# A cross-attention's maximum pass moved into its key and value projection

## The chip, the cores and the metric

The kernel runs on one core of a Trainium2 chip. The metric is device microseconds (us) of one execution. TensorE (PE) multiplies matrices, VectorE (DVE), ScalarE (ACT) and GpSimd (POOL) work elementwise, SyncE (SP) issues most DMAs. Each engine takes its instructions in order, and engines wait for each other by semaphores.

## The reference, cut to what matters

Three layers on a stream x of 256 tokens by 512: cross-attention to a context of 4096 tokens, grouped self-attention, and a gated feed-forward layer. The change touches the first, and nothing of what the others compute:

```python
q = _qdq(x) @ _qdq(wq).T + bq                 # 256 x 512, int8 fake-quantized
kv = cond @ wkv.T + bkv                        # cond: 4096 x 512; wkv: 1024 x 512
k, v = jnp.split(kv, 2, axis=-1)               # 16 heads of 32
attn = jax.nn.softmax(jnp.einsum('bnhd,bmhd->bhnm', q, k) * scale, axis=-1)
o = jnp.einsum('bhnm,bmhd->bnhd', attn, v).reshape(B, N, C)
out = _qdq(o) @ _qdq(wp).T + bp
```

The result must keep nearly full fp32 precision. So each fp32 operand is split into a high part (fp32r, which TensorE multiplies in one pass) and a low part, and a product is three passes: high by high, high by low, low by high (`three_pass`).

## The kernel before, in words

**Stage A, keys and values.** The context comes in eight chunks of 512 tokens (`context_chunk`). ScalarE rounds a chunk to its high part (`high`), VectorE subtracts for the low part (`low`). TensorE projects four groups g of 128 key channels (four heads each; 12 matmuls of 512 columns each, PSUM banks 0 and 1), then four tiles mt of 128 tokens of values (12 matmuls each, banks 2 and 3). ScalarE writes the high part of the keys (L639), VectorE the low part (`k_low`, L878); both go to a scratch in DRAM, `kh_dram` and `kl_dram`. The values stay in SBUF as `v_all`, head by head (L653). During chunk 1 the queries are prepared: x is normalized and quantized, wq and wp are quantized in halves on VectorE (`quantize_weight_half`), transposed on TensorE, and the queries projected, split (`split_queries`) and stored.

**Stage B, sixteen heads.** For head h the high keys, low keys and high keys again are loaded from the scratch as three times 32 rows into one of two `k_stack` buffers, so that one matmul of 96 rows does the three passes at once (`load_k`); two rows of ones below them take the negated row maximum. The queries are loaded to `q_max` and `q_stack` in the same way.
- The maximum pass (`maximum_pass`, L1214): 16 matmuls a head, of 96 rows by 512 columns, queries on the output's partitions, into banks 4 and 5; VectorE reduces each (`chunk_maxima`, L918). It runs one head ahead, in pairs of tiles between the other matmuls. For head 0 it is spread over stage A.
- `negate_maximum`, `maximum_rows` (TensorE turns it into two rows, bank 7) and `maximum_row` (VectorE writes them to `q_stack`, L953).
- `scores` (L1307): eight chunks c of 512 keys, each four matmuls of 98 rows by 256 columns, keys on the output's partitions, into banks 0 and 1 or 2 and 3. ScalarE takes the exponential of a whole chunk, 128x1024, to a ring of four (`p_ring`, L681).
- `values` (L1319): four matmuls side by side in four column groups of 32, bank 6, from `v_head`, a copy of the head's values that a DMA makes of `v_all`.
- The softmax's denominators: GpSimd adds chunks 1, 2, 4, 5 and 6 to chunk 0 (`sum_chunks`, L563); TensorE multiplies chunks 3 and 7 and that sum by ones (`denominators`, L1331).
- ScalarE copies bank 6 out (L670), TensorE merges the four column groups (`merge`, L1293 and L1295), VectorE divides (`normalize_output`).

The order of the matmuls in a head is written out by hand in `head`: for i of 0 to 3, two maximum tiles, scores(2i), scores(2i+1), two maximum tiles, at i = 1 the merge of the head before, at i = 3 the maximum rows of the next one, then the values of the two chunks before.

An fp32 matmul stands in the trace as two records; an fp32r one as one.

Of the kernel before, what the change touches and what calls it, by code (L numbers as in the profile page):

```python
# [35 lines left out]
P = 128  # L36
# [10 lines left out]
SUM_CHUNKS = (0, 1, 2, 4, 5, 6)  # L47
NSUMS = len(SUM_CHUNKS) - 1
SUMS_BEFORE = (-2, -1, 0, None, 1, 1, 2, None)
# [23 lines left out]

FF_UNITS = 4
NSTREAM = FF0 + 3 * FF_UNITS

# [32 lines left out]
def perceiver(nc, x_in, stream, wq_in, wp_in, bias_cols, bias_rows, out):  # L109
    with ExitStack() as ctx:  # L110
# [17 lines left out]
        x_hat = sb("x_hat", [P, NT, D], F32)  # L128
# [17 lines left out]
        m_part = sb("m_part", [P, CHUNKS, NT], F32)  # L146
        neg_m = sb("neg_m", [P, NT], F32)
        neg_hl = sb("neg_hl", [P, NT, 2], F32)
# [5 lines left out]
        s_inv = sb("s_inv", [P, 2, NT], F32)  # L154


        with ExitStack() as ab:
            v_all = sb("v_all", [P, H, MT, DH], F32, ab)
            with ExitStack() as prep:
                w_raw = sb("w_raw", [P, 2, D], F32, prep)  # L160
                w_q = [sb(f"w_q{i}", [P, KT, D], BF16, prep) for i in range(2)]
                wq_t = sb("wq_t", [P, KT, D], BF16, prep)
                ones = sb("ones", [P, P], F32, prep)
                diag = sb("diag", [P, KT, P], F32, prep)
                sx_row = sb("sx_row", [P, N], F32, prep)
                in_q = sb("in_q", [P, NT, D], BF16, prep)
                in_t = sb("in_t", [P, KT, N], BF16, prep)
                w_amax = sb("w_amax", [P, KT], F32, prep)
                w_inv = sb("w_inv", [P, KT], F32, prep)
                wq_s = sb("wq_s", [P, KT], F32, prep)  # L170
                wp_s = sb("wp_s", [P, KT], F32, prep)

            k_stack = [sb("k_stack0", [P, M], F32R, ab)]
            q_max = [sb("q_max0", [P, N], F32R, ab)]
            q_stack = [sb("q_stack0", [P, N], F32R, ab)]
            q_max.append(sb("q_max1", [P, N], F32R, ab))
            q_stack.append(sb("q_stack1", [P, N], F32R, ab))
            v_head = [sb("v_head0", [P, MT, DH], F32, ab)]
            with ExitStack() as a:
# [5 lines left out]
                kl_buf = sb("kl_buf", [P, KT, D], F32R, a)  # L185
            with ExitStack() as b:
# [38 lines left out]
        def bank(i):  # L225
            return ps[:, i, :]


        wkv_raw = v_all[:].rearrange("p h m d -> p (h m d)")[:, 0:2 * KT * D].rearrange(
            "p (w k n) -> p w k n", w=2, k=KT)  # L230
        bp_row = swp_row
        q_f = diag[:, 0:NT, :].rearrange("p t n -> p (t n)")

# [1386 lines left out]
```

## Time and profile before

| | us |
|---|---|
| median of three runs | 686.84 (686.0 to 687.2) |
| the profiled execution: its time | 683.01 |
| its span, first to last instruction | 681.2 |
| busy in the span: TensorE | 619.2 |
| VectorE | 411.6 |
| ScalarE | 291.5 |
| GpSimd | 240.9 |

Mean granted TensorE clock: 0.962 of full speed. A group in the profile is all instructions of one line, engine, operation and form; its mean is of one instruction with its latency, so pipelined matmuls add up to more than their busy time. "idle" ahead of an instruction names the work that ended the wait. The lines L326 to L328 are the three passes of `three_pass`.

### The profile page before, as it was taken

The numbers are of one execution on the slowest core, as the hardware profiler recorded it, in microseconds if no ns is written. First come the engines' busy times: TensorE is split into PE (matmuls) and PEld (weight loads), VectorE is DVE, ScalarE is ACT, GpSimd is POOL, SyncE is SP. The second block draws the span as 40 slices with busy tenths as digits, with TensorE's granted clock in tenths as the row PEclk, the third lists the DMA queues.
The fourth block names the chain that finished last, engine by engine and source line by source line (L and its number), as shares of the span: only waits on it lengthen the run. The fifth ranks groups of instructions, "written<-read, shape, count | busy, mean of one in ns | idle before, by whom it ended". The sixth has DMA issues, their size and how long they took to land.

```text
span 681.2 us, 12389 instructions
## 1 busy us (share of the span) xinstructions
PE 619.2 (91%) x4324; PEld 479.7 (70%) x4324; DVE 411.6 (60%) x721; ACT 291.5 (43%) x392; POOL 240.9 (35%) x125
## 2 busy tenths in 40 slices
PE   5999999999999999999999999985796879779998
PEld 3877788888866666666666666653686768669997
DVE  3796432223347777777777777732478786765552
ACT  3444233323315455555444555452154446444441
POOL 1000200000026666777777777773002433230000
PEclk9999999999999999999999999976697999879999
DMA  8663644365294555555555555301031123125520
GB/s 301 242 228 131 221 147 147 123 209 170 99 278 117 138 135 146 151 142 137 145 145 145 143 141 136 85 8 55 1 125 62 63 98 150 62 74 201 184 99 31
DMA packets 29757, 92.17 MB, mean 135 GB/s; under 512 B 5472, under 2 KB 9568, under 8 KB 23008
## 3 DMA queue, kind: packets, MB, share of 16 engines
q1 hardware_dynamic: 28480, 89.67, 43.1%
q10 hardware_dynamic: 1248, 2.10, 0.8%
q8 instruction: 19, 0.31, 0.2%
q14 instruction: 10, 0.08, 0.0%
HBM read 65.02 MB, written 18.35 MB: 122 GB/s over the span
## 4 chain that ended last, share of the span: by engine, by line
PE 74%; DVE 12%; issue 6%; ACT 5%; POOL 1%; DMA 1%; SPq 0%; ACTq 0%; POOLq 0%; DVEq 0%
PE ps L326 13%; PE ps L327 13%; PE ps L328 13%; PE ps L1214 10%; PE ps L1319 9%; PE ps L1307 8%; PE ps L1331 3%; ACT p_ring L681 3%; DVE s_max L1046 1%; DVE s_bias L1048 1%; POOL p_sum L563 1%; DVE probs L1043 1%; PE ps L1293 1%; DVE probs L1054 1%; PE ps L1295 1%
## 5 line engine op out<-in xcount | busy, mean ns | idle before, releaser
L918 DVE TENSOR_REDUCE m_part<-ps 128x1 f32<-128x512 f32 (+1 forms) x256 | 165.4, 686 | 92.2 <-PE ps L1214 86.6
L681 ACT ACTIVATE p_ring<-ps 128x1024 f32<-128x1024 f32 x128 | 124.6, 1024 | 100.7 <-PE ps L1307 100.7
L563 POOL TENSOR_TENSOR p_sum<-p_sum,p_ring 128x1024 f32<-128x1024 f32 x64 | 152.6, 2384 | 13.4 <-ACT p_ring L681 9.2
L1214 PE MATMUL ps<-k_stack,q_max 96*128 96x512 f32 (+1 forms) x256 | 98.4, 439 | 3.4 <-DVE m_part L918 1.3
L1307 PEld LDWEIGHTS ps<-q_stack,k_stack 98*128 98x128 f32 x512 | 71.2, 191 | 18.6 <-ACT p_ring L681 11.3
L1307 PE MATMUL ps<-q_stack,k_stack 98*128 98x256 f32 x512 | 76.9, 288 | 7.8 <-ACT p_ring L681 7.8
L1319 PE MATMUL ps<-p_ring,v_head 128*32 128x256 f32 x1024 | 75.7, 391 | 0.1
L1214 PEld LDWEIGHTS ps<-k_stack,q_max 96*128 96x128 f32 x256 | 42.6, 188 | 42.7 <-issue 22.7
L326 PE MATMUL ps<-xt_h,h_ring 128*128 128x256 f32 x208 | 60.9, 293 | 2.2 <-DVE xt_l L1017 2.1
L563 POOL TENSOR_TENSOR p_sum<-p_ring 128x1024 f32<-128x1024 f32 x16 | 38.0, 2373 | 70.2 <-ACT p_ring L681 70.2
L878 DVE SCALAR_TENSOR_TENSOR kl_buf<-ps,biases,kh_buf 128x512 fp32r<-128x512 f32 x32 | 23.9, 749 | 61.3 <-ACT kh_buf L639 60.9
L327 PE MATMUL ps<-xt_l,h_ring 128*128 128x256 f32 x208 | 60.6, 291 | 0.0
L328 PE MATMUL ps<-xt_h,l_ring 128*128 128x256 f32 x208 | 60.4, 291 | 0.0
L326 PE MATMUL ps<-h_ring,wkv_h 128*128 128x512 f32 x128 | 52.0, 406 | 8.7 <-DVE l_ring L838 8.1
L309 DVE TENSOR_TENSOR l_ring<-f_ring,h_ring 128x2048 fp32r<-128x2048 f32 x22 | 51.7, 2354 | 12.6 <-ACT h_ring L305 12.5
L327 PE MATMUL ps<-l_ring,wkv_h 128*128 128x512 f32 x128 | 50.8, 397 | 0.0
L328 PE MATMUL ps<-h_ring,wkv_l 128*128 128x512 f32 x128 | 50.8, 397 | 0.0
L326 PE MATMUL ps<-wkv_h,h_ring 128*128 128x512 f32 x128 | 50.1, 391 | 0.0
L328 PE MATMUL ps<-wkv_h,l_ring 128*128 128x512 f32 x128 | 49.9, 390 | 0.0
L327 PE MATMUL ps<-wkv_l,h_ring 128*128 128x512 f32 x128 | 49.9, 390 | 0.0
L589 POOL TENSOR_TENSOR l_ring<-f_ring,h_ring 128x2048 fp32r<-128x2048 f32 x7 | 32.0, 4572 | 44.5 <-ACT h_ring L741 31.7
L653 ACT COPY v_all<-ps 128x512 f32 (+1 forms) x32 | 18.8, 587 | 67.0 <-PE ps L328 67.0
(174 smaller groups left out, 1034.7 us busy)
## 6 DMA issues: line engine op xcount, KB each, us to landing
f_ring<-stream SPq DMA_DIRECT2D x29, 1024.0 KB, 4.9
k_stack<-kh_scratch SPq DMA_DIRECT2D x60, 256.0 KB, 4.6
kh_scratch<-kh_buf SPq DMA_DIRECT2D x32, 256.0 KB, 5.6
kl_scratch<-kl_buf SPq DMA_DIRECT2D x32, 256.0 KB, 6.2
v_head<-v_all SPq DMA_DIRECT2D x16, 512.0 KB, 3.0
k_stack<-kl_scratch SPq DMA_DIRECT2D x30, 256.0 KB, 4.2
v_all<-stream SPq DMA_DIRECT2D x4, 256.0 KB, 4.9
f_ring<-stream SPq DMA_DIRECT2D x4, 256.0 KB, 5.6
```

What stands on the lines that cost most here:

```text
L309: nc.vector.tensor_tensor(l_ring[which][:], f_ring[which][:], h_ring[which][:].bitcast(F32), ALU.subtract).then_inc(l_ready, 1)
L326: nc.tensor.matmul(out_ap, lh, rh, start=start, stop=False)
L327: nc.tensor.matmul(out_ap, lh, rl, start=False, stop=False)
L328: return nc.tensor.matmul(out_ap, ll, rh, start=False, stop=stop)
L563: nc.gpsimd.tensor_tensor(p_sum[:, p, :], p_ring[:, 0, :] if n == 0 else p_sum[:, p, :], p_ring[:, c % 4, :], ALU.add).then_inc(sums_done, 1)
L589: nc.gpsimd.tensor_tensor(l_ring[w][:], f_ring[w][:], h_ring[w][:].bitcast(F32), ALU.subtract).then_inc(l_ready, 1)
L681: nc.scalar.activation(p_ring[:, c % 4, :], ps[:, 2 * (c % 2):2 * (c % 2) + 2, :].rearrange("p b n -> p (b n)"), ACT.Exp, scale=XSCALE).th ...
L878: nc.vector.scalar_tensor_tensor(out=kl_buf[:, g, :], in0=bank(g % 2), scalar=biases[:, KT + g:KT + g + 1], in1=kh_buf[:, g, :].bitcast(F3 ...
L918: nc.vector.reduce_max(m_part[:, mc0 + j // NT, j % NT:j % NT + 1], bank(4 + j % 2), AX.X).then_inc(max_read, 1)
L1214: nc.tensor.matmul(bank(to), q_max[p][0:SPLIT_ROWS, at128(j % NT)], k_stack[p][0:SPLIT_ROWS, k_at], start=True, stop=True).then_inc(max_do ...
L1307: last = nc.tensor.matmul(ps[:, 2 * (c % 2) + k // 2, (k % 2) * N:(k % 2 + 1) * N], k_stack[p][0:SPLIT_ROWS + MAX_ROWS, at128(4 * c + k)], ...
L1319: last = nc.tensor.matmul(bank(6)[k * DH:(k + 1) * DH, 0:N], v_head[p][:, 4 * c + k, :], p_ring[:, c % 4, k * N:(k + 1) * N], start=c == 0 ...
```

## The change

- The maximum pass leaves stage B. In stage A there are now 64 sets: for chunk c, group g of four heads and query tile t, twelve matmuls of 32 rows by 512 columns, three passes over four heads; head i takes partitions 32i to 32i+31 of the keys and queries as they lie in SBUF, and bank 4 + i. One maximum on VectorE reads the four banks. A set waits for the maximum of the set before.
- Stage A is a list of half steps (6 matmuls): values of chunks 0 and 1, then keys of chunks 0, 1 and 2, and from there values and keys in turn. `SETS_AFTER` says after which of the 112 half steps a set stands: the first sixteen after steps 5 to 16 and 18 to 21, the rest from 23 on nearly evenly, most of them two steps apart.
- The low parts of the context from chunk 2 on, and that of the keys' weights, move from VectorE to GpSimd.
- wq is quantized before the key steps, wp between maxima in steps 24 to 38, and wp is transposed after step 45.
- In stage B, VectorE adds chunks 0 to 6 (six adds, `add_chunk`), and TensorE makes denominators of chunk 7 and the sum only. `v_all` is laid out token tile first and read by `values` directly; `v_head` and its loads are gone, and so are `q_max` and its loads. Output accumulates in bank 6 or 4 in turn. The maximum rows of head h+1 are made at i = 2, and VectorE copies them to `q_stack` behind its sixth add.
- Loops over chunks and heads on TensorE are unrolled.

```diff
-SUM_CHUNKS = (0, 1, 2, 4, 5, 6)
-NSUMS = len(SUM_CHUNKS) - 1
-SUMS_BEFORE = (-2, -1, 0, None, 1, 1, 2, None)
+NSUMS = 6
+SUMS_BEFORE = (-2, -1, 0, None, 1, 1, 2, 3)
...
+SETS = KT * NT
+FIRST_SETS = (5, 6, 7, 8, 9, 10, 11, 12, 13, 14, 15, 16, 18, 19, 20, 21)
+STEPS = 2 * KT * (2 * NCTX - 2)
+WP_STEP = 45
...
+def step_before_set(m):
+
+    if m < len(FIRST_SETS):
+        return FIRST_SETS[m]
+    c, g = m // SETS, m % SETS // NT
+    even = 23 + (m - 16) * (STEPS - 24) // (SETS * NCTX - 17)
+    return max(even, first_step_of_keys(c) + 2 * g + 3)
...
+            def context_low(s, w):
+                pool.wait_ge(h_ready, s + 1)
+                pool.wait_ge(l_ready, s)
+                nc.gpsimd.tensor_tensor(l_ring[w][:], f_ring[w][:], h_ring[w][:].bitcast(F32),
+                                        ALU.subtract).then_inc(l_ready, 1)
...
+            def set_maxima(m):
+                c, g, t = m // SETS, m % SETS // NT, m % NT
+                dve.wait_ge(max_done, m + 1)
+                nc.vector.reduce_max(m_part[:, c, t, g * HPG:(g + 1) * HPG], ps[:, 4:8, :], AX.X).then_inc(max_read, 1)
...
+            for step in range(STEPS):
+                kind, c, g, half = step_of(step)
+                if kind == "k" and half == 1:
                     k_low(c, g)
...
+                if step == 3:
+                    split_queries()
+                for m in SETS_AFTER[step]:
+                    set_maxima(m)
...
+            def add_chunk(h, p, c):
+
+                dve.wait_ge(exp_done, 8 * h + c + 1)
+                if c == 1:
+                    wait(dve, sums_used, h - 1)
+                else:
+                    dve.wait_ge(sums_done, NSUMS * h + c - 1)
+                nc.vector.tensor_tensor(p_sum[:, p, :], p_ring[:, 0, :] if c == 1 else p_sum[:, p, :],
+                                        p_ring[:, c % 4, :], ALU.add).then_inc(sums_done, 1)
+
+            def head(h, p):
+
+                first, last = (isinstance(h, int) and h == n for n in (0, H - 1))
+                for c in range(1, 4):
+                    add_chunk(h, p, c)
                 if not first:
                     normalize_output(h - 1)
...
+                add_chunk(h, p, 4)
                 if not first:
                     output_maximum(h - 1)
...
+                for c in range(5, 7):
+                    add_chunk(h, p, c)
+                if not last:
                     maximum_row(h + 1, 1 - p)
...
+            def maximum_set(m):
+
+                c, g, t = m // SETS, m % SETS // NT, m % NT
+                pe.wait_ge(kl_evac, 4 * c + g + 1)
+                if m == 0:
+                    pe.wait_ge(ql_ready, KT)
+                wait(pe, max_read, m)
+                for n, (q, k) in enumerate(((q_nat_h, kh_buf), (q_nat_h, kl_buf), (q_nat_l, kh_buf))):
+                    for i in range(HPG):
+                        rows = slice(i * DH, (i + 1) * DH)
+                        last = nc.tensor.matmul(bank(4 + i), q[rows, g, at128(t)], k[rows, g, :],
+                                                start=n == 0, stop=n == 2)
+                last.then_inc(max_done, 1)
...
+            def head(h, p):
 
                 for i in range(4):
...
+                    scores(h, p, 2 * i)
+                    scores(h, p, 2 * i + 1)
+                    if i == 1 and h > 0:
                         merge(h - 1)
-                    if i == 3 and next_loads is not None:
+                    if i == 2 and h < H - 1:
                         maximum_rows(h + 1)
                     if i > 0:
-                        values(h, p, loads, 2 * i - 2)
-                        values(h, p, loads, 2 * i - 1)
-                    elif not first:
-                        values(h - 1, 1 - p, None, CHUNKS - 2)
-                        values(h - 1, 1 - p, None, CHUNKS - 1)
+                        values(h, p, 2 * i - 2)
+                        values(h, p, 2 * i - 1)
+                    elif h > 0:
+                        values(h - 1, 1 - p, CHUNKS - 2)
+                        values(h - 1, 1 - p, CHUNKS - 1)
```

## Rows read from the trace of the kernel before

**Rows 1.** The page: busy us of TensorE, share of the span, instructions.

```profile
PE 619.2 (91%) x4324; PEld 479.7 (70%) x4324; DVE 411.6 (60%) x721; ACT 291.5 (43%) x392; POOL 240.9 (35%) x125
```

**Rows 2.** Windows of stage A and B: length, then busy us of each engine.

```profile
core 0: us, PE busy (x) PEld busy (x) DVE busy (x) ACT busy (x) POOL busy (x), PEclk, DMA share, GB/s
64.00:203.99 139.99, 137.97 (x603) 112.19 (x602) 50.23 (x67) 40.16 (x54) 7.04 (x2) 1.00 0.55 173
222.35:434.96 212.61, 205.56 (x1926) 138.44 (x1925) 156.29 (x326) 107.45 (x119) 154.63 (x65) 1.00 0.54 141
```

**Rows 3.** TensorE's timeline in stage A; 48 matmuls lie between the starts.

```profile
22.73 0.39 PE L326 MATMUL ps<-wkv_h,h_ring 128*128 128x512 f32 x1
...
33.61 0.39 PE L326 MATMUL ps<-h_ring,wkv_h 128*128 128x512 f32 x1
```

**Rows 4.** ScalarE's timeline over one head (start, us, what, idle before).

```profile
304.38 2.88 ACT L681 ACTIVATE p_ring<-ps 128x1024 f32<-128x1024 f32 x3
309.72 1.94 ACT L681 ACTIVATE p_ring<-ps 128x1024 f32<-128x1024 f32 x2 [2.45 <-PE ps L1307]
...
320.75 1.03 ACT L681 ACTIVATE p_ring<-ps 128x1024 f32<-128x1024 f32 x1
```

**Rows 5.** VectorE's timeline: query split (first, last), a maximum row, the last normalization.

```profile
63.19 0.48 DVE L865 SCALAR_TENSOR_TENSOR diag<-ps,wq_s,sx_row 128x256 f32<-128x256 f32 x1 [1.73 <-PE ps L1206]
...
68.39 0.48 DVE L871 SCALAR_TENSOR_TENSOR o_all<-diag,biases,x_hat 128x256 fp32r<-128x256 f32 x1
...
315.51 0.43 DVE L953 CAST q_stack<-ps 2x256 fp32r<-2x256 f32 x1
...
468.98 0.17 DVE L958 RECIPROCAL r_den<-ps 128x2 f32<-128x2 f32 x1 [10.90 <-PE ps L1295]
```

**Rows 6.** TensorE's timeline inside one head.

```profile
308.39 0.73 PE L1214 MATMUL ps<-k_stack,q_max 96*128 96x512 f32 x2
308.96 1.12 PE L1307 MATMUL ps<-q_stack,k_stack 98*128 98x256 f32 x8
309.92 0.85 PE L1214 MATMUL ps<-k_stack,q_max 96*128 96x512 f32 x2
310.70 1.07 PE L1319 MATMUL ps<-p_ring,v_head 128*32 128x256 f32 x16
...
318.26 1.07 PE L1319 MATMUL ps<-p_ring,v_head 128*32 128x256 f32 x16
...
320.13 0.74 PE L1214 MATMUL ps<-k_stack,q_max 96*128 96x512 f32 x2
```

**Rows 7.** Groups by form: count, busy us, mean ns of one, idle before.

```profile
L918 DVE TENSOR_REDUCE m_part<-ps 128x1 f32<-128x512 f32 x244 | 157.1, 686 | 66.9 <-PE ps L1214 61.3
L589 POOL TENSOR_TENSOR l_ring<-f_ring,h_ring 128x2048 fp32r<-128x2048 f32 x7 | 32.0, 4572 | 44.5 <-ACT h_ring L741 31.7 <-ACT h_ring L305 12.7
L346 DVE TENSOR_REDUCE w_amax<-w_raw 128x2 f32<-128x1024 f32 x2 | 2.4, 1213 | 0.0
L887 DVE TENSOR_TENSOR wkv_l<-v_all,wkv_h 128x2048 fp32r<-128x2048 f32 x1 | 2.3, 2291 | 1.0 <-ACT wkv_h L643 1.0
L910 DVE TENSOR_TENSOR x_cur<-x_cur,swp_row 128x512 f32<-128x512 f32 x2 | 1.4, 692 | 0.1
```

**Rows 8.** Windows, columns as in rows 2; PEclk is the granted clock.

```profile
452.00:458.00 6.00, 6.00 (x39) 4.09 (x43) 4.46 (x5) 2.51 (x3) 4.22 (x3) 0.50 0.01 3
508.00:512.00 4.00, 1.98 (x16) 1.61 (x16) 3.45 (x11) 2.19 (x8) 0.00 (x0) 1.00 0.00 2
```

**Rows 9.** TensorE's timeline in the last head, with idle time before.

```profile
448.84 0.64 PE L1331 MATMUL ps<-p_sum,ones_col 128*32 128x256 f32 x8 [0.94 <-POOL p_sum L563]
...
451.11 0.80 PE L1307 MATMUL ps<-q_stack,k_stack 98*128 98x256 f32 x4 [0.97 <-ACT p_ring L681]
...
455.20 2.08 PE L1307 MATMUL ps<-q_stack,k_stack 98*128 98x256 f32 x8
```

**Rows 10.** Groups of weight loads by form, columns as in rows 7.

```profile
L1214 PEld LDWEIGHTS ps<-k_stack,q_max 96*128 96x128 f32 x256 | 42.6, 188 | 42.7 <-issue 22.7 <-DVE m_part L918 18.9 <-DMA k_stack<-kh_scratch 0.4
L1319 PEld LDWEIGHTS ps<-p_ring,v_head 128*32 128x32 f32 x1024 | 31.5, 110 | 20.1 <-issue 8.0 <-ACT p_ring L681 1.1
```

More of the change, by code:

```diff
@@ new lines, in next_chunk_high @@
+            def next_chunk_high(c):
+                act.wait_ge(k_done, 4 * min(c, 2))
+                act.wait_ge(v_done, 4 * c)
+                high(act, c + 3, slot(c + 3), uses(c + 3))
+            high(act, CTX0 + 1, 1, 1)
+            for mt in range(4):
+                evacuate_values(0, mt)
+            act.wait_ge(wk_loaded, 16)
+            nc.scalar.copy(wkv_h[0][:], wk_raw).then_inc(h_ready, 1)
+            evacuate_values(1, 0)
+            evacuate_values(1, 1)
+            evacuate_tokens(0, in_t)
@@ L908, in _ @@
-            dve.wait_ge(rows_loaded, 32)
-            for t in range(NT):
-                order.step(nc.vector.tensor_tensor(x_cur[:, t, :], x_cur[:, t, :], bp_row[:], ALU.add))
-            weight_and_token_rows()
-            split_queries()
-            def chunk_maxima(h, first, last, mc0=0):
-                for j in range(first, last):
-                    dve.wait_ge(max_done, 16 * h + 2 * mc0 + j + 1)
-                    nc.vector.reduce_max(m_part[:, mc0 + j // NT, j % NT:j % NT + 1], bank(4 + j % 2),
-                                         AX.X).then_inc(max_read, 1)
@@ L1209, in project_queries @@
                         last.then_inc(q_done, 1)
-            def maximum_tile(j, to, k_at, p, before):
-                wait(pe, max_read, before - 1)
-                nc.tensor.matmul(bank(to), q_max[p][0:SPLIT_ROWS, at128(j % NT)], k_stack[p][0:SPLIT_ROWS, k_at],
-                                 start=True, stop=True).then_inc(max_done, 1)
-            def maximum_pass(h, p, loads, first, last):
-                for j in range(first, last):
-                    if j == 0:
-                        pe.wait_ge(qm_loaded[p], 48 * loads)
-                    if j % 8 == 0:
-                        pe.wait_ge(ks_loaded[p][j // 8], 48 * (loads - 1 + p))
-                    maximum_tile(j, 4 + j % 2, slice(j // NT * D, (j // NT + 1) * D), p, 16 * h + j)
@@ new lines, in _ @@
+            transpose_wq()
+            split_chunk(CTX0 + 1)
+            for step in range(STEPS):
+                kind, c, g, half = step_of(step)
+                if kind == "k":
+                    if c >= 2 and g == 0 and half == 0:
+                        split_chunk(c + CTX0)
+                    project_keys(c, g, half)
+                else:
+                    project_values(c, g, half)
+                if step == 1:
+                    project_queries()
+                for m in SETS_AFTER[step]:
+                    maximum_set(m)
+                if step == WP_STEP:
+                    prepare_wp(sum(len(sets) for sets in SETS_AFTER[:step + 1]))
+                if step == STEPS - 4:
+                    maximum_rows(0)
@@ L1375, in _ @@
+            pe.wait_ge(ones_set, 3)
+            pe.wait_ge(max_read, SETS * NCTX)
+            for h in range(H):
+                head(h, h % 2)
             for c in (CHUNKS - 2, CHUNKS - 1):
-                values(H - 1, 1, None, c)
-            pe.wait_ge(o_done, NT * (H - 1))
+                values(H - 1, 1, c)
             merge(H - 1)
```

586 lines of the change are left out of this document (248 added, 338 removed).

## The prediction

> **What bounds the kernel now.** I read the page first, then the windows by stage, then TensorE's timeline at the start and the three engines' timelines inside one head, then the groups by form, for what one instruction costs, and last the granted clock where TensorE idles. TensorE is busy 619.2 of 681.2 us [rows 1], but the stages differ. Stage A (keys and values, up to the first scores at 203.99) is projection back to back: TensorE busy 137.97 of 139.99 us [rows 2]; 48 matmuls of 512 columns take 10.88 us, 0.227 us each [rows 3]. Stage B (sixteen heads) is also TensorE's, 205.56 of 212.61 us, with VectorE at 156.29, ScalarE at 107.45 and GpSimd at 154.63 [rows 2]. A head repeats every 16.37 us (exponentials at 304.38 and 320.75, [rows 4]). The last normalization of stage B is at 468.98 [rows 5], so B lasts 265.0 us. What follows, 212 us, is unchanged. So the question is what A gains in length and what B loses.
>
> In a head, two chunks of scores cost 0.96 us, two maximum tiles before them 0.57, two before values 0.78, and two chunks of values with two sets of denominators 1.87 [rows 6]. The 16 tiles are thus some 5.5 to 6 us, the rest some 10.4.
>
> **Stage B after.** Gone are the maximum tiles, one of three denominator sets (0.4 us), the loads of q_max and v_head (hidden today) and GpSimd's adds. TensorE keeps about 10 us per head, ScalarE eight exponentials at 0.97 and a copy, 8.3. VectorE gets six adds of 128x1024. Between 692 ns for 512 and 2291 for 2048 elements [rows 7] an add is 1.22 us; each waits for the one before, so 1.24. With the normalization (0.75), the output maximum (0.25) and the maximum row (0.43, [rows 5]) that is 8.9 us: less than TensorE's, but it is a chain. Two SBUF operands are taken at the same rate in both of these rows, so I see no reason for an add outside 1.14 (next to no wait) to 1.36. The new wait is that scores(h+1, 0) needs maximum_row(h+1), which now stands behind add 6 of head h on VectorE. By hand, from the start of scores(h, 0) as 0:
> - exponential 0 starts at 0.75 (308.96 to 309.72, [rows 4, 6]), exponential 1 ends at 2.67;
> - TensorE does both scores, the old head's last values and denominators by 2.9, scores 2 follow, and exponential 2 runs from 3.65 to 4.61, behind the copy;
> - VectorE: add 2 at 4.67, add 3 to 7.1, normalization to 7.9, add 4 to 9.1, maximum, add 5 to 10.6, add 6 to 11.8 (exponential 6 ended at 9.8), maximum row to 12.25.
>
> The next scores start at 12.3. Fifteen such periods and 14.2 us for the last head up to its normalization are 198.7 us: B loses 66. Behind the wait stand the old head's last values, so TensorE idles some 2.2 us in each head (10.05 to 12.3). Bounds: 10.7 if the row came free (TensorE and ScalarE taking turns), 13.0 if an add costs 1.36. DMA is hidden: today's 55% of 16.37 us is 9 us, under 12.3 even with nothing removed.
>
> **Stage A after.** The 96 matmuls of the two value chunks end at 33.61 as today's first chunk does [rows 3]; I add 1.1 for the low part of chunk 1, 2.0 for transposes and 1.2 until wq is rounded: the key steps start at 37.9 (36 to 40). A half step is 6 x 0.227 = 1.36 us.
> - Steps 0 to 5 and the query projection: 9.9, to 47.8. Queries are split after the second low part of the keys, from 46.2, for 5.7 us (63.19 to 68.88, [rows 5]), so the first set waits until 52.0.
> - A set is 12 matmuls of 32 rows, in three rounds over four row groups, into banks 4 to 7, and one maximum of 4 x 512 elements. By 686 ns for 512 and 1213 for 1024 [rows 7] that takes 2.27 us. The banks are single: matmuls of set m+1 wait for the maximum of set m, and behind that wait, in TensorE's queue, stands the next half step of the projection, and so the evacuations and the key stores that follow it. Four matmuls into four column groups do run side by side today: 16 records in 1.07 us [rows 6]. If row groups do too, a round costs 0.227, the set occupies TensorE 0.68 plus 0.17 for changing shape (0.78 against 0.57, [rows 6]), 0.85; from release to last result it is 1.04.
> - So sets follow each other no faster than 1.04 + 0.06 + 2.27 + 0.07 = 3.44 (0.06 and 0.07 are my estimate of what passes between two engines). With one half step between them TensorE has only 2.21 us of work: 1.2 is idle. Sets 0 to 16: 14 such gaps and 2 of two steps (3.6) are 55.4, to 107.4.
> - Sets 16 to 63 (the schedule's own list): 40 gaps of two steps at 3.6, six tight at 3.44, one of three at 4.95, the last set 1.05: 170.6, to 278.0.
> - Preparing wp with its two copies in line 4, wp's rounding between maxima 2, last maximum 2.3: scores start near 286, not 204. A grows by 82.
>
> The low parts that move to GpSimd (4.57 us each, [rows 7]) and to ScalarE's copy have a chunk of over 40 us to hide in; without that cover each would be 4.6. The values' copy keeps its size and only its order of writing changes: nothing. SP's queue loses 48 small loads of q_max, the sixteen of v_head and their waits; k_stack for head h+2 has a head and a half to land, 16 us and more, so its queue is no bound. Writing the query parts to q_nat_h and q_nat_l instead of two older buffers is the same work: nothing.
>
> Two tiles before column groups cost 0.2 us more than two before full-array scores [rows 6]. The Trainium skill, TensorE Tiling, Tiling Modes, says why: TensorE drains when the tiling mode changes. The sets make 128 such changes; by that rule and this row they would be 26 us against my 11, and the sum 744.
>
> **The clock.** The granted clock was 1.00 through stage B, but in the last head it stood at 0.50 (1.2 of 2.4 GHz) from 452 to 458 [rows 8], after idle gaps of 0.94 and 0.97 us a little apart [rows 9]; it held from 508 to 512, where TensorE was busy 1.98 us of 4 [rows 8]. The new 2.2 us idle of every head lie between these two. At half clock eight scores take 2.08 instead of 1.12 [rows 6, 9]. A fall right behind the gap of 3.5 to 6.8 us doubles up to 2.9 us of TensorE work before exponential 2, and with it the chain: 1.75 to 3.2, so 2.4. I take 11 of 16 heads: 26 us (bounds 0 and 51).
>
> **Sum, against the profiled execution's 683.01 us:** +82 - 66 + 26 = +42, 725; the runs' median is 3.8 higher, so 729.
>
> **Rivals.**
> 1. *Loads in single file.* A 32-column load takes 110 ns, one of 128 columns 188, though it has 96 rows and not 128 [rows 10]: 0.81 ns per column, 0.104 us for 128, and nothing for rows. If loads of different row groups queue, 12 x 0.107 (with a little for the start) = 1.28: TensorE 1.45 per set, 1.75 to the result, tight gaps 4.15, double 4.25. Sets 0 to 16 take 66.5, sets 16 to 63 202.2, scores start at 329, A grows by 125: 683 + 125 - 66 = 742, or 746 as a median; 772 with clock falls. For it: each set brings 12 full-width loads for 0.68 us of streaming. Against: nothing here shows loads queueing at that rate.
> 2. *Clock holds*, as in 508 to 512: 683 + 82 - 66 + 4 = 703. For it: a head is still 10 us of work in 12.3.
> 3. *No overlap at all* between row groups: 12 x 0.227 = 2.73 per set, 64 x 1.9 = 121 more: 824 and up. The column groups speak against it.
> 4. *Faster: the heads get short.* If the maximum row is not late, because adds keep up with the exponentials, a head is 10.7 and the idle gap goes, the clock with it: 16 x 1.6 = 26 below rival 2, 677. It decides from a head under 11.2 us (16 us / 16) with sets at 0.85. For it: VectorE has only 8.9 us of work. Against: add 3 to the maximum row is an unbroken row of steps.
>
> TensorE: Matmul & The Clock Gate, Part 3, in the Trainium skill, reports 3.07 times for four row tiles of 512 columns. By that a round would be 4 x 0.227 / 3.07 = 0.30, and 64 sets 13 us more, an estimate; no run here shows it yet.
>
> **Chances.** Forecast 0.34 (own range 712 to 745); clock holds 0.17, of which 0.03 lands within 0.2%; loads in file 0.28; no overlap 0.04; faster 0.17. A difference of 0.2% is about what a measurement of this kernel can tell from none. Faster 0.17, same 0.03, slower 0.80. Range 680 to 775: it leaves out no overlap, the worst of rival 1 and the better half of rival 4.
>
> **What would show it.** Scores first start near 286 (330 under rival 1). Starts of four matmuls of a set 0.06 us apart, rounds 0.23 apart (0.43 under rival 1, 0.9 under rival 3). The maximum: near 2.27 us, and TensorE waiting for it some 1.2 us per set early on. Heads 12.3 apart at full clock, over 14 with falls; scores waiting for the maximum row (L953's successor) about 2 us per head; granted clock below 1.00 in stage B. The prediction is wrong if sets overlap with their own loads even less, if the idle gap does not lower the clock, or if adds run faster than 1.24.

## The result: 751 us instead of 687

| | us |
|---|---|
| before, median of 4 runs | 686.66 (686.0 to 687.2) |
| after, median of 4 runs | 750.88 (748.31 to 754.47) |
| ratio, 95% interval | 1.094 (1.088 to 1.100) |
| predicted | 729 (680 to 775), slower with 0.80 |

The profiled execution of after has a span of 746.5 us. The windows cut it at the first scores (before 203.99 [rows 2], now 313.21) and at the last normalization of stage B (before 468.98 [rows 5], now 535.16); those within stage A set apart the start, the first sets, and the stop from 165 to 177 in which TensorE prepares wp:

```profile
core 0: us, PE busy (x) PEld busy (x) DVE busy (x) ACT busy (x) POOL busy (x), PEclk, DMA share, GB/s
0.00:57.80 57.80, 40.05 (x174) 30.61 (x174) 36.13 (x55) 19.57 (x27) 12.96 (x24) 0.94 0.51 186
57.80:116.00 58.20, 45.80 (x312) 29.25 (x312) 44.07 (x27) 9.59 (x11) 9.15 (x2) 0.97 0.38 135
116.00:165.00 49.00, 44.71 (x284) 30.02 (x276) 41.27 (x38) 8.85 (x13) 4.60 (x1) 1.00 0.26 84
165.00:177.00 12.00, 8.97 (x44) 5.74 (x45) 2.38 (x2) 3.57 (x5) 0.00 (x0) 0.72 0.00 0
177.00:313.21 136.21, 127.24 (x797) 86.89 (x795) 93.74 (x62) 27.03 (x36) 21.97 (x5) 1.00 0.35 113
313.21:535.16 221.95, 190.03 (x1980) 130.22 (x1980) 136.38 (x176) 135.29 (x145) 0.00 (x0) 0.91 0.45 107
535.16:746.50 211.34, 175.69 (x1127) 156.77 (x1128) 135.56 (x210) 88.90 (x157) 38.68 (x21) 0.92 0.27 97
```

Stage A grew by 109 us, stage B shrank from 265 to 222, the rest kept its 211 to 212. TensorE, busy 619.2 us before [rows 1], is busy 632.5 now, and idle 52 us more. The longer busy time is not more work: with the same instructions and a granted clock of 0.99 instead of 0.91 in stage B, run 1 below is busy 619.6 us. The page says where the idle time is:

```profile
L885 DVE TENSOR_REDUCE m_part<-ps 128x4 f32<-128x2048 f32 x64 | 146.5, 2289 | 60.8 <-PE ps L1228 60.7
L973 DVE TENSOR_TENSOR p_sum<-p_sum,p_ring 128x1024 f32<-128x1024 f32 x80 | 98.0, 1225 | 32.6 <-ACT p_ring L677 28.2
L1315 PE MATMUL ps<-q_stack,k_stack 98*128 98x256 f32 x512 | 86.0, 316 | 33.6 <-DVE q_stack L899 30.5
```

TensorE waited 30.5 us before scores (L1315) for VectorE's copy of the maximum row (L899): the wait that the prediction put at 2.2 us a head. One head, first TensorE, then VectorE (start, us, what, idle before):

```profile
353.24 1.22 PE L1315 MATMUL ps<-q_stack,k_stack 98*128 98x256 f32 x8 [2.12 <-DVE q_stack L899]
...
366.07 1.99 PE L1315 MATMUL ps<-q_stack,k_stack 98*128 98x256 f32 x8 [2.12 <-DVE q_stack L899]
```

```profile
356.15 1.23 DVE L973 TENSOR_TENSOR p_sum<-p_ring 128x1024 f32<-128x1024 f32 x1 [2.97 <-ACT p_ring L677]
358.31 2.48 DVE L973 TENSOR_TENSOR p_sum<-p_sum,p_ring 128x1024 f32<-128x1024 f32 x2 [0.94 <-ACT p_ring L677]
360.83 0.17 DVE L955 RECIPROCAL r_den<-ps 128x2 f32<-128x2 f32 x1
...
361.50 1.22 DVE L973 TENSOR_TENSOR p_sum<-p_sum,p_ring 128x1024 f32<-128x1024 f32 x1
362.65 0.21 DVE L963 TENSOR_REDUCE a_part<-o_all  x1
363.07 2.48 DVE L973 TENSOR_TENSOR p_sum<-p_sum,p_ring 128x1024 f32<-128x1024 f32 x2 [0.21 <-DVE a_part L963]
365.59 0.43 DVE L899 CAST q_stack<-ps 2x256 fp32r<-2x256 f32 x1
```

The last line is what scores wait for, and everything above it from 358.31 on is a row of steps with no wait over 0.21 us. Scores start 12.83 us after those of the head before when the clock holds; before the change a head repeated every 16.37 [rows 4]. Both idle gaps are 2.12 us, but behind the second eight scores take 1.99 us and not 1.22: half clock (1.2 of 2.4 GHz), and the next copy comes 14.37 us later (379.96). Windows behind the first gap and behind the second show it in PEclk, the last but two of the figures:

```profile
353.00:357.00 4.00, 3.76 (x46) 2.71 (x47) 1.03 (x2) 2.52 (x3) 0.00 (x0) 1.00 0.47 98
366.00:370.00 4.00, 3.93 (x32) 2.73 (x36) 0.56 (x2) 1.94 (x2) 0.00 (x0) 0.57 0.45 94
```

Of the fourteen distances between the rows of heads 1 to 15, six are 12.5 to 12.8, seven 14.4 and one 15.8.

Then stage A. Two sets that are two half steps apart (a double gap), and two that are one apart (a tight gap):

```profile
233.72 0.50 PE L1228 MATMUL ps<-kh_buf,q_nat_h 32*128 32x512 f32 x4
234.06 0.40 PE L1228 MATMUL ps<-kl_buf,q_nat_h 32*128 32x512 f32 x4
234.30 0.40 PE L1228 MATMUL ps<-kh_buf,q_nat_l 32*128 32x512 f32 x4
234.62 0.50 PE L355 MATMUL ps<-wkv_h,h_ring 128*128 128x512 f32 x1
...
237.62 0.50 PE L1228 MATMUL ps<-kh_buf,q_nat_h 32*128 32x512 f32 x4
```

```profile
69.57 0.51 PE L1228 MATMUL ps<-kh_buf,q_nat_h 32*128 32x512 f32 x4 [0.90 <-DVE m_part L885]
...
73.02 0.51 PE L1228 MATMUL ps<-kh_buf,q_nat_h 32*128 32x512 f32 x4 [0.89 <-DVE m_part L885]
```

A line with x4 is one round over four heads, and the rounds start 0.34 and 0.24 us apart: four matmuls run in the time of one. The double gap is 3.90 (3.89 over many), the tight one 3.45 with 0.9 idle.

### The profile page after: what moved, and what is told of

Read it like the earlier page. It is cut to its first block, busy times and chain, and to the rows that moved or that the text cites. A ratio compares the mean times of both kernels' runs of the same rounds, so it can differ in the third digit from the quotient of the medians.

```text
span 746.5 us, 12075 instructions
## 1 busy us (share of the span) xinstructions
PE 632.5 (85%) x4707; PEld 469.5 (63%) x4708; DVE 489.5 (66%) x565; ACT 292.8 (39%) x392; POOL 87.4 (12%) x53
## 4 chain that ended last, share of the span: by engine, by line
PE 54%; DVE 28%; issue 10%; ACT 4%; DMA 2%; DVEq 1%; ACTq 0%; POOL 0%; SPq 0%
PE ps L355 12%; PE ps L356 11%; PE ps L357 11%; PE ps L1228 7%; DVE m_part L885 7%; PE ps L1315 6%; DVE p_sum L973 6%; PE ps L1327 4%; ACT p_ring L677 2%; PE ps L1339 2%; DMA x_cur<-x_in 2%; DVE probs L1055 1%; DVE s_max L1047 1%; DVE s_bias L1049 1%; DVE probs L1044 1%
## 5 line engine op out<-in xcount | busy, mean ns | idle before, releaser
L885 DVE TENSOR_REDUCE m_part<-ps 128x4 f32<-128x2048 f32 x64 | 146.5, 2289 | 60.8 <-PE ps L1228 60.7
L973 DVE TENSOR_TENSOR p_sum<-p_sum,p_ring 128x1024 f32<-128x1024 f32 x80 | 98.0, 1225 | 32.6 <-ACT p_ring L677 28.2
L1315 PE MATMUL ps<-q_stack,k_stack 98*128 98x256 f32 x512 | 86.0, 316 | 33.6 <-DVE q_stack L899 30.5
L1315 PEld LDWEIGHTS ps<-q_stack,k_stack 98*128 98x128 f32 x512 | 71.9, 208 | 61.8 <-DVE q_stack L899 37.7
L1327 PE MATMUL ps<-p_ring,v_all 128*32 128x256 f32 x1024 | 82.8, 423 | 0.0
L625 ACT ACTIVATE kh_buf<-ps,biases 128x512 fp32r<-128x512 f32 x32 | 22.0, 688 | 125.5 <-PE ps L357 125.5
L619 ACT COPY v_all<-ps 128x512 f32<-128x512 f32 x32 | 18.8, 586 | 97.8 <-PE ps L357 97.8
L1228 PE MATMUL ps<-kh_buf,q_nat_h 32*128 32x512 f32 x256 | 32.3, 491 | 26.2 <-DVE m_part L885 21.7
L973 DVE TENSOR_TENSOR p_sum<-p_ring 128x1024 f32<-128x1024 f32 x16 | 19.6, 1226 | 49.6 <-ACT p_ring L677 49.6
L334 ACT CAST h_ring<-f_ring 128x2048 fp32r<-128x2048 f32 x23 | 43.8, 1906 | 9.3 <-PE ps L357 7.2
L1327 PEld LDWEIGHTS ps<-p_ring,v_all 128*32 128x32 f32 x1024 | 33.1, 117 | 19.8 <-issue 4.8
```

Source lines behind the costliest of these rows:

```text
L334: nc.scalar.copy(h_ring[which][:], f_ring[which][:]).then_inc(h_ready, 1)
L625: nc.scalar.activation(kh_buf[:, g, :], bank(g % 2), ACT.Identity, bias=biases[:, KT + g:KT + g + 1]).then_inc(kh_evac, 1)
L885: nc.vector.reduce_max(m_part[:, c, t, g * HPG:(g + 1) * HPG], ps[:, 4:8, :], AX.X).then_inc(max_read, 1)
L973: nc.vector.tensor_tensor(p_sum[:, p, :], p_ring[:, 0, :] if c == 1 else p_sum[:, p, :], p_ring[:, c % 4, :], ALU.add).then_inc(sums_done, 1)
L1228: last = nc.tensor.matmul(bank(4 + i), q[rows, g, at128(t)], k[rows, g, :], start=n == 0, stop=n == 2)
L1315: last = nc.tensor.matmul(ps[:, 2 * (c % 2) + k // 2, (k % 2) * N:(k % 2 + 1) * N], k_stack[p][0:SPLIT_ROWS + MAX_ROWS, at128(4 * c + k)], ...
```

## The experiments

Runs 3 to 8 were executed once each. The changed kernel's own four times lie between 748.3 and 754.5, and in the four profiled executions whose stage A is that of the changed kernel (it, runs 1, 2 and 8) the first scores start between 313.21 and 316.10. So a difference of some 3 us in either, in a single run, shows nothing.

**1. The row earlier.** On VectorE one call moves:

```diff
                 if not first:
                     normalize_output(h - 1)
+                if not last:
+                    maximum_row(h + 1, 1 - p)
                 add_chunk(h, p, 4)
...
-                if not last:
-                    maximum_row(h + 1, 1 - p)
```

> One line moves: on VectorE the copy of the next head's maximum row stands right behind the normalization, before add 4, and no longer behind add 6. Nothing is left out. My theory (the scores of head h+1 wait for this row, and the idle gap of about 2 us that this makes lowers the clock): the row is there some 4 us before it is wanted, TensorE and ScalarE take turns, heads come 10.5 to 11 us apart instead of 12.6 and 14.4 in turn, the granted clock stays at 1.00 through the heads, stage B takes 15 x 10.7 + 14.2 = 175 us instead of 222, and the whole about 704. Rival 1 (the wait only moves: the last denominators of head h still need add 6, and TensorE idles there instead): heads about 12, stage B about 194, the whole about 723, clock still below 1.00. Rival 2 (the clock falls for another cause than the gap): heads 11 but with half-clock stretches, stage B about 195. Stage A unchanged in all: first scores at about 313.

Measured: 707.8 us (706.8 to 709.0), ratio to before 1.032 (1.027 to 1.037). The rows are 11.3 apart at first and 10.86 from the fourth on, and stage B, from 316.10 to 493.54, is 177.4 us. Its window:

```profile
316.10:493.54 177.44, 175.70 (x1980) 121.85 (x1980) 137.54 (x176) 135.05 (x145) 0.00 (x0) 0.99 0.57 133
```

(For the changed kernel the same window has 190.03 of 221.95 us and a clock of 0.91.) TensorE is idle for 1.7 of 177 us, and the granted clock is 0.99. So the order on VectorE alone costs 43 us; rival 1 (the wait only moves) and rival 2 (another cause of the clock) both fall.

**2. The gap filled.** Seven matmuls without use in the place of the wait:

```diff
+                    if i == 3 and h < H - 1:
+                        wait(pe, o_done, NT * h)
+                        for _ in range(7):
+                            nc.tensor.matmul(bank(7), h_ring[0][:, 0, 0:P], h_ring[0][:, 1, :], start=True,
+                                             stop=True)
```

> The wait for the maximum row stays, but TensorE gets seven matmuls of 512 columns (1.6 us, results unused, into a free bank) in each head behind values 5, where it now idles for 2.1 us. Nothing is left out, work is added. Theory (the gap lowers the clock, and that is what parts heads of 14.4 us from heads of 12.6): granted clock 1.00 in the heads, all heads 12.3 to 12.8 apart, stage B about 203 instead of 222, the whole about 732, although TensorE does 26 us of work more. Rival (the clock falls for another reason, or the clock is not what makes every second head long): heads stay at 12.6 and 14.4, or get longer by up to 1.6, the whole 751 to 775. Stage A unchanged.

(Their operands are a chunk for the second layer, waited for before the first head.) Measured: 735.9 us, 15 less than the changed kernel although TensorE gets 15 x 7 x 0.2325 = 24 us of work more.

```profile
402.54 1.91 PE L1364 MATMUL ps<-h_ring 128*128 128x512 f32 x7
404.73 1.22 PE L1315 MATMUL ps<-q_stack,k_stack 98*128 98x256 f32 x8 [0.28 <-DVE q_stack L899]
```

Scores still start when the row comes, the rows are 12.83 apart in nearly every head, and stage B has a granted clock of 0.99. The idle gap lowers the clock, and the clock is worth 15 us. What is left between this run and the one before (28 us; 15 heads by 12.83 - 10.86 are 29.6) is the wait itself.

**3. Another order in the set.** The two loops of `maximum_set` change places:

```diff
-                for n, (q, k) in enumerate(((q_nat_h, kh_buf), (q_nat_h, kl_buf), (q_nat_l, kh_buf))):
-                    for i in range(HPG):
+                for i in range(HPG):
+                    for n, (q, k) in enumerate(((q_nat_h, kh_buf), (q_nat_h, kl_buf), (q_nat_l, kh_buf))):
```

> The two loops of a set are swapped: the three passes of one head (one row group) follow each other, then the next head, so that neighbouring matmuls mostly share their row group; same number, shape and banks. Nothing is left out. Theory (matmuls of different row groups run side by side, those of one row group do not): the three passes of a head take 0.68 us, only the borders between heads overlap, a set occupies TensorE for 2.1 to 3.0 us instead of 1.16, double gaps grow from 3.89 to about 5.3, tight gaps from 3.46 to about 5.0, and the first scores start 60 to 110 us later, at 375 to 425. Rival (what overlaps is only the load with the matmul, and the four banks, not row groups): nothing changes, first scores at 313. Stage B unchanged in both.

Measured: 754.1 us, first scores at 318.13. My theory expected 375 to 425 and is wrong. (Of the 4.9 us against 313.21, 1.5 lie in the start, 1.5 in one gap of 5.89 instead of 4.35, which run 8 has too, and the rest in sets that are 0.02 to 0.05 longer.)

```profile
232.79 0.53 PE L1228 MATMUL ps<-kh_buf,q_nat_h 32*128 32x512 f32 x4
233.12 0.43 PE L1228 MATMUL ps<-kl_buf,q_nat_h 32*128 32x512 f32 x4
233.35 0.43 PE L1228 MATMUL ps<-kh_buf,q_nat_l 32*128 32x512 f32 x4
233.71 0.50 PE L355 MATMUL ps<-wkv_h,h_ring 128*128 128x512 f32 x1
```

The first matmuls of all four heads still start together, although two other matmuls of the first head stand ahead of that of the second in the program. A set takes 0.92 us from its start to the next projection (0.90 in the other order). Whether the row groups matter at all was now open.

**4. One row group.** All twelve matmuls read rows 0 to 31:

```diff
-                        rows = slice(i * DH, (i + 1) * DH)
+                        rows = slice(0, DH)
```

> All twelve matmuls of a set read rows 0 to 31 of the keys and queries, one row group, and still write four banks: three quarters of the maxima are left out (those of the first head of each group are taken four times). Number, shape, loads and banks are as in the changed kernel. Theory (the matmuls run side by side because they stand in four row groups; the order of issue did not matter): they now run one behind the other, a set takes 12 x 0.227 = 2.7 us and more, double gaps grow from 3.89 to 5.5 to 6, tight gaps from 3.46 to 5.2 to 5.6, first scores at 415 to 435, the whole about 855 to 870. Rival (what makes four run at once is that they are short of rows, or write four banks): double gaps stay at 3.89, first scores at 313, the whole 750. In between (a set of 1.3 to 2 us): loads overlap, streams do not.

Measured: 940.9 us, first scores at 506.84. From TensorE's timeline, and the window up to the copy of the first maximum row, 6 us before the scores:

```profile
303.55 1.19 PE L1228 MATMUL ps<-kh_buf,q_nat_h 32*128 32x512 f32 x4
304.59 1.07 PE L1228 MATMUL ps<-kl_buf,q_nat_h 32*128 32x512 f32 x4
305.50 1.08 PE L1228 MATMUL ps<-kh_buf,q_nat_l 32*128 32x512 f32 x4
306.51 0.80 PE L355 MATMUL ps<-wkv_h,h_ring 128*128 128x512 f32 x1
307.10 0.63 PE L356 MATMUL ps<-wkv_l,h_ring 128*128 128x512 f32 x1
```

```profile
0.00:500.83 500.83, 475.81 (x1587) 338.85 (x1587) 215.28 (x178) 68.08 (x89) 48.25 (x32) 0.79 0.22 76
```

The set takes 2.96 us instead of 0.90: with loads, shapes and four banks unchanged, what makes four matmuls run side by side is that they stand in four row groups. The mechanism and the size of the set (2.7 "and more") are as expected. The total is 70 us past my range, because behind many such sets the projection runs at half clock (0.43 us from matmul to matmul behind 307.10): the granted clock up to 500.83 is 0.79, with TensorE busy 476 of 501 us. Double gaps are 5.9 us where the clock holds, as expected (5.5 to 6), and 7.5 where it has fallen. I had not priced that.

**5. Full rows.** A set of four matmuls with the projection's own shape:

```diff
+                for i in range(HPG):
+                    last = nc.tensor.matmul(bank(4 + i), q_nat_h[:, g, at128(t)], (kh_buf, kl_buf)[i % 2][:, g, :],
+                                            start=True, stop=True)
```

> A set is four matmuls of 128 rows x 512 columns, of the same shape as the projection's, instead of twelve of 32 rows: the four banks then hold no head's scores, so the real maxima are left out. Streaming time 4 x 0.23 = 0.92 us against 3 x 0.23 = 0.69 in the set of the change, which occupies TensorE for 1.16. Theory (0.3 to 0.5 us of a set are the two changes between 128-row and 32-row matmuls): a set of full rows costs 0.92 and no changes, so double gaps get shorter than 3.89, 3.64 to 3.7, and the 40 of them about 9 us. Rival 1 (a set pays for something other than the shape, its start on new banks or its wait): double gaps get longer, 3.89 + 0.23 = 4.1. Tight gaps stay at 3.46 in both (the maximum's).

Measured: 745.3 us. Most double gaps are 3.71 to 3.73, tight ones 3.64. The lines at a set:

```profile
233.01 0.40 PE L1226 MATMUL ps<-kh_buf,q_nat_h 128*128 128x512 f32 x1
...
233.70 0.40 PE L1226 MATMUL ps<-kl_buf,q_nat_h 128*128 128x512 f32 x1
233.93 0.40 PE L355 MATMUL ps<-wkv_h,h_ring 128*128 128x512 f32 x1
```

Sixteen matmuls of one shape at 0.2325 are 3.72: no cost beyond the columns. The real set has three rounds, 0.70, but takes 3.89 - 12 x 0.2325 = 1.10. So 0.40 us of each set, 26 us of 64, go to the two changes of shape. That it is not the four row groups getting in each other's way is seen in run 4, whose twelve matmuls run one by one: the starts on either side of a change are 0.33 to 0.34 apart there too, and all others 0.23. I was wrong on the tight gaps: the maximum waits for a set that is 0.2 longer, and they grow with it.

**6. A shorter maximum.** VectorE reads a quarter of each bank (`ps[:, 4:8, 0:P]`).

> VectorE's maximum of a set reads 128 of the 512 columns of each bank: it leaves three quarters of the maxima out. It should take about 0.7 us instead of 2.29. Theory (the tight gaps of 3.46 are the maximum's, the double gaps of 3.89 are TensorE's: two half steps 2.72 and the set 1.16): tight gaps fall to 2.5 (1.36 + 1.16), double gaps stay at 3.89, about 20 tight gaps and the wait around the preparation of wp give 19 to 23 us, first scores at 290 to 294, the whole about 730. Rival 1 (the single banks or VectorE set the double gaps too): they fall as well, by up to 0.5 us each, first scores near 270. Rival 2 (the set itself costs TensorE less than it seems, since it only waits): tight gaps fall to 2.2 or less. Stage B unchanged.

Measured: 727.0 us, first scores at 288.75; the maximum takes 0.69.

```profile
232.94 0.69 DVE L885 TENSOR_REDUCE m_part<-ps 128x4 f32<-128x512 f32 x1 [1.34 <-PE ps L1228]
...
236.84 0.69 DVE L885 TENSOR_REDUCE m_part<-ps 128x4 f32<-128x512 f32 x1 [0.84 <-PE ps L1228]
```

Double gaps stay at 3.90, tight gaps are 2.97 and 2.03 in turn, 2.5 on average. Tight gaps are VectorE's, double ones TensorE's. Some 20 of them and the stop for wp gave 24 us.

**7. VectorE and GpSimd at the start.** Set 0 stood at 58.63 and not at 52.0. VectorE, then GpSimd, in the changed kernel:

```profile
25.87 4.68 DVE L385 TENSOR_SCALAR v_all<-v_all 128x512 f32<-128x512 f32 x1
30.59 3.70 DVE L387 TENSOR_SCALAR v_all<-v_all 128x512 bf16<-128x512 f32 x1
```

```profile
25.51 4.76 POOL L541 TENSOR_TENSOR wkv_l<-v_all,wkv_h 128x2048 fp32r<-128x2048 f32 x1 [5.95 <-ACT wkv_h L638]
30.40 3.61 POOL L544 MEMSET k_stack<- 32x4096 f32 x1
```

```diff
+            dve.wait_ge(h_ready, CTX0 + 2)
+            nc.vector.tensor_tensor(wkv_l[0][:], wk_raw, wkv_h[0][:].bitcast(F32), ALU.subtract).then_inc(l_ready, 1)
...
                 context_low(s, slot(s))
+                if s == CTX0 + 2:
+                    pool.wait_ge(ones_set, 1)
+                    pool.wait_ge(l_ready, CTX0 + 3)
+                    nc.gpsimd.memset(k_stack[0][SPLIT_ROWS:P, :].bitcast(F32), 1.0).then_inc(ones_set, 1)
```

> Two pieces of GpSimd work leave the stretch in which VectorE prepares the queries and weights: the low part of the key weights (4.76 us on GpSimd at 25.51) goes to VectorE, between the diagonals and the weights' scales (2.3 us there), and the filling of the ones rows of k_stack0 (3.61 us at 30.40) stands behind the first low part of a context chunk. Nothing is left out. Theory (VectorE's steps at 25.87 and 30.59 took 4.68 and 3.70 us instead of 0.43 because GpSimd ran beside them): both take about 0.43 again, transposes of the tokens are 5 to 6 us earlier, the idle gap of 5.5 us on TensorE before 34.35 and its half clock go, key steps start at 38 to 40 instead of 43.8, the queries are split and the first set starts at 52 to 54 instead of 58.6, first scores at 306 to 309, the whole about 745. Rival (the long steps wait for data, a transfer or something of their own): they stay near 4 us, and the 2.3 us more on VectorE make the first set later, 60 to 61, the whole 752 to 754.

Measured: 749.9 us. Both steps are short again:

```profile
26.13 0.43 DVE L385 TENSOR_SCALAR v_all<-v_all 128x512 f32<-128x512 f32 x1
26.59 0.43 DVE L387 TENSOR_SCALAR v_all<-v_all 128x512 bf16<-128x512 f32 x1
```

So the cause is shown: VectorE stood still while GpSimd's instruction ran, and each step ended 0.3 us after GpSimd's. The Trainium skill (SBUF — State Buffer, SBUF: two separate sides) has the rule: the two engines share a pair of ports that one of them holds for a whole instruction; VectorE wants it in a 2-port perf mode, or with two SBUF inputs against a GpSimd instruction that reads SBUF. The trace agrees that the wait lasts for the whole instruction (4.76 and 3.61 us); in which mode a step ran, no run here shows. Only 2.0 us come out at the first scores (311.22), not 4 to 7, and the total can't show so little. TensorE still waits, for wq (2.70) and as before for the split queries (4.45), behind one VectorE step too many. The 2.0 also understate the repair: in this execution GpSimd's first step on the tokens (L519) stood at 19.34 and not at 17.77, so everything behind the tokens began 1.6 us late.

**8. The adds back on GpSimd.** With them the copy of the maximum row goes right behind the normalization, and TensorE's merge waits for the normalization of the head before.

```diff
+            for h in range(H):
+                for c in range(1, 7):
+                    pool.wait_ge(exp_done, 8 * h + c + 1)
...
+                    nc.gpsimd.tensor_tensor(p_sum[:, h % 2, :], p_ring[:, 0, :] if c == 1 else p_sum[:, h % 2, :],
+                                            p_ring[:, c % 4, :], ALU.add).then_inc(sums_done, 1)
```

> The six adds of the chunks in a head go back to GpSimd, everything else of the change stays; the copy of the next head's maximum row then stands right behind the normalization on VectorE. Nothing is left out. What my account of the heads says: GpSimd's add takes 2.38 us, as before the change, six in a chain 14.3 us, with handoffs 14.6 to 16; the row is never late, the gap before the scores goes, and TensorE instead waits for the sums before the last denominators. Heads 14.6 to 16 us apart, stage B 235 to 255 instead of 222, the whole 760 to 785: moving the adds was worth some 15 to 35 us, less than what the order on VectorE gives (the run with the row earlier: 43). Rival (the length of a head comes from the other parts, the scores' exponentials and TensorE, and the adds have slack on GpSimd): heads 11 to 12, the whole about 710. Stage A unchanged.

Measured: 783.4 us; heads 15.3 apart on average, but mostly 12 and 17 to 19 in turn, and the granted clock from the first scores to the last normalization is 0.83. GpSimd, then TensorE's longest wait in a head:

```profile
380.79 12.41 POOL L570 TENSOR_TENSOR p_sum<-p_sum,p_ring 128x1024 f32<-128x1024 f32 x5 [0.30 <-ACT p_ring L688]
```

```profile
393.26 1.08 PE L1346 MATMUL ps<-p_sum,ones_col 128*32 128x256 f32 x8 [3.98 <-POOL p_sum L570]
```

Six adds in a row take GpSimd 14.8 us, so its chain alone makes heads long; how much of the rest is the clock was not taken apart. VectorE's adds, with their late row, are 32 us better than six adds on GpSimd, clock included, and with an early row 76. (Before, GpSimd had five.)

**9. Five repairs together.** Runs 1 and 7, queries split one key tile earlier (`if step == 1`), TensorE waiting for the prepared wp only at the next set (wp's transposes stand one half step later for it), and the wait for the last maximum moved from the first scores to the first values.

> Five small repairs of what the runs before showed, nothing left out: the maximum row stands right behind the normalization (707.8 us by itself); the low part of the key weights on VectorE and the ones rows filled later (first scores 2 us earlier by itself); the queries are split right behind the first low part of the keys and not the second (the first set waited 4.45 us for them); TensorE waits for the prepared wp only before the next set (an interval of 11.9 us between two maxima where 3.9 is usual); the wait for the last maximum stands before the first values and no longer before the first scores (2.45 us idle). My account (these waits add up, each is on TensorE's path): 707.8 - 2 - 4.4 - 5 - 3 = 693, first scores at 300 to 303, heads 10.86 apart. Rival (stage A is held by the maxima and not by TensorE, so an earlier start and a shorter stop are lost again in later tight gaps): first scores at 306 to 309, the whole 698 to 702. Against the kernel before, 686.7: slower by 1 to 2 per cent in both.

Measured: 689.6 us, ratio to before 1.007 (1.004 to 1.010). First scores at 298.52; the interval at wp is 7.06 instead of 11.91. All of the gain arrives, and some 3 us more. It lies in the start: the first maximum stands at 51.27, 10.9 us before that of run 1 (62.20), where 2 and 4.4 had been reckoned.

**10. Stage A in quarters.** The list of half steps becomes one of quarters (`.`), sets (`|`) and the rest (W, Q, P: wq, queries, wp; H: next chunk's high part; R: row of head 0). It was laid out with prices from the traces: 0.70 a quarter, 1.10 a set, 2.29 a maximum.

```diff
+PROGRAM = ("k00.... k01.... k02.W... k03.Q...H v13.... k10.|..|. v20..|.. v21.|...| k11...|. k12..|.. "
...
-                for kt in (2 * half, 2 * half + 1):
+                for kt in (quarter,):
```

> The repairs of the row, the low part and the last wait as in the combined run, and stage A in another order, nothing left out: the projection goes in quarters (three matmuls, 0.70 us) instead of halves of a tile, key and value tiles alternate in an order written out by hand, one value tile of chunk 1 stands behind the keys of chunk 0, and a set comes wherever VectorE is about to be free (every 3 or 4 quarters). Arithmetic, banks and buffers are those of the change. My account (tight gaps cost 0.94 us of idle TensorE each, 20 of them, because a half step of 1.36 us and a set do not fill 3.46; with quarters 3 x 0.70 + 1.16 = 3.25 nearly does): adding up quarters at 0.70, sets at 1.10 and maxima at 2.29 in this order gives the first scores at 287 and some 21 us of idle left, the whole 707.8 - (316.1 - 287) = 679, 1 per cent below the kernel before. Rival (stores, conversions of the next chunk or evacuations, which the halves had time for, now come late, or each change between tile shapes costs more than 1.10 allows): first scores at 295 to 305, the whole 687 to 697, no gain over the kernel before.

Measured: 676.3 us (675.8 to 680.0), ratio to before 0.987 (0.984 to 0.990): 1.3 per cent faster than the kernel before. First scores at 286.62. Windows of its three stages:

```profile
0.00:286.62 286.62, 263.65 (x1600) 180.70 (x1601) 213.86 (x184) 67.79 (x89) 43.85 (x31) 1.00 0.38 129
286.62:462.83 176.21, 174.56 (x1981) 120.86 (x1979) 136.87 (x173) 135.42 (x146) 0.00 (x0) 1.00 0.60 141
462.83:675.50 212.67, 175.31 (x1128) 156.61 (x1128) 137.58 (x210) 88.41 (x157) 38.71 (x21) 0.92 0.27 97
```

From set 30 on nearly every maximum starts 3.45 or 3.46 behind the last. There stage A is held by the chain of set and maximum over single banks; at 3.46 a set, 64 sets would be 221 us of it.

## Why the prediction was right, and where it was off

Slower was right, and by the mechanism named: A had to grow by more than B lost, because a set and its maximum follow each other over the same four banks. The 22 us that are missing are all in A. The number alone would not show it: 751 lies outside the forecast's own range (712 to 745) and nearer to rival 1's 746. What speaks for the forecast is its mechanism, row by row.

| term | predicted | measured |
|---|---|---|
| first maximum starts | 53.1 | 60.05 |
| sets 0 to 16 | 55.4 | 56.8 |
| sets 16 to 63, with wp | 169.6 + 6 | 193.9 |
| first scores | 286 | 313.21 |
| stage B with the clock | 198.7 + 26 | 222.0 |
| the rest | 212 | 211.3 |

- **The start (+7).** "The key steps start at 37.9 (36 to 40)"; they started at 43.8. The step that failed is that low parts on GpSimd have cover and cost nothing. They had it, but that of the key weights (4.76 us), and the filling of the ones rows behind it (3.61), stopped VectorE, which had none (run 7). I had asked what hides GpSimd's work, and not whom it slows. The half clock that the idle gap left on TensorE belongs to it.
- **Tight gaps.** 3.44 predicted, 3.45 measured; the maximum 2.27 and 2.29. Right, and run 6 shows that they are VectorE's.
- **Double gaps (+8).** 3.6 predicted, 3.89 measured, in 29 of the 47 distances from set 16 on. The rounds were right (0.227 predicted), the change of shape was not: 0.17 a set against 0.40 (run 5). The Trainium skill, TensorEngine Tiling (Array Packing), Tiling Modes, has the rule that a change of tiling mode drains TensorE. The trace agrees. The prediction's estimate with that rule, 26 us for 128 changes by its rows on column groups, is what 64 x 0.40 give; its sum took 11. Of these 26 only what falls into double gaps costs time.
- **Odd gaps and wp (+10).** Eleven distances are neither tight nor double, 57.0 us with the one at wp. At 3.6 each and one 4.95 they would be 41; the 6 us set aside for wp cover less than half of the rest. At wp the interval is 11.91, 8.0 over a double one: TensorE waited 2.49 for a maximum, did the transposes, waited for their copies and then ran four microseconds at half clock. The others lie where a set waits for the low part of its own keys or for wp's rounding, and I took apart only one. In the gap of 5.62 behind 135.92 the step that failed at the start fails again: GpSimd's low part runs from 136.01 for 4.60 us, and a VectorE step of 0.17 us for wp (L374, 139.37) takes 1.27 and ends with it.
- **Stage B (-3), by two errors that cancel.** A head at full clock is 12.83 and not 12.3: VectorE's chain is as long as worked out, to 0.1 us, but it starts 5.07 behind the scores (358.31 to 353.24) and not 4.67. The clock costs 15 us and not 26: it falls in about eight of the heads, and a fall costs 1.55, not 2.4 (run 2). Run 1 shows that both hang on one wait.
- **Rival 1** (loads in single file): refuted, rounds are 0.24 apart and not 0.43. (Its double gap should have been 2 x 1.36 + 1.45 = 4.17 and not 4.25, some 3 us less.) **Rival 3** (no overlap) is what run 4 made: 941 us. **Rival 2** (the clock holds) is run 2, and did not come by itself. **Rival 4** had the condition right (heads under 11.2), and one moved call brings 10.86; but it needed sets at 0.85 as well, so even then the kernel is 3 per cent slower than before.
- The rule that four row tiles give 3.07 times (the Trainium skill, TensorE: Matmul & The Clock Gate, Part 3) would make a round 0.30. The trace disagrees for rounds that follow each other within a set (0.24) and lies near it for a whole set: 2.96 / 0.90 = 3.3.

## What to carry to other kernels

Work that is moved to an idle engine must be priced twice: its own time, and what it does to the engine beside it. Where a product and its reduction pass through one set of banks, their sum is a period, and the work between two of them should be cut into pieces that fill it; here quarters instead of halves, with keys and values in turn, turned 0.7 per cent slower into 1.3 per cent faster, the new order taken as a whole. And a result that another engine waits for goes ahead of the work that only a later step needs: one line, 43 us.

## What was not expected of the hardware

- The order in which matmuls of different row groups are issued made no difference (0.92 and 0.90 us a set): in the trace the fourth head's first matmul starts with the first head's, ahead of six that stand before it in the program. So "each engine takes its instructions in order", as said at the beginning, does not hold for TensorE's starts across row groups.
- The granted clock fell to its lower level (1.2 GHz) behind sets of twelve matmuls in one row group, with TensorE busy throughout: 17.00 of 17 us from 229 to 246, clock 0.80. With four row groups it stays at 1.00 (177 to 313, TensorE busy 127 of 136).
- The same idle gap of 2.12 us left the clock at 1.00 once (353.24) and at half the next time (366.07), nearly in turn.
- VectorE's steps of 0.43 us took 4.68 and 3.70 beside one instruction of GpSimd each, and in run 1 a step on 128x2 elements (L374, 0.17 us elsewhere) took 3.92.
